# The low half of the shared expert's inner units, made by VectorE in place of GpSimd

## The reference, cut to what matters

```python
# xf: all tokens, layer-normalised; 512 inner values per token
sg = xf @ shared_gate_w.T
su = xf @ shared_up_w.T
shared_out = silu(sg) * su @ shared_down_w.T
# beside it, for each token: 16 scores -> 2 of 4 groups -> 4 experts and their weights
topk_idx, w, _scores = _route(xf, router_w, correction_bias)
```

## Time and profile before

| what | us |
|---|---|
| median of 3 runs | 3146.3 |
| lowest, highest | 3137.9, 3148.9 |
| the profiled execution | 3140.2 |
| its span | 3138.3 |
| PE busy | 2709.5 (86%) |
| VectorE busy | 2195.0 (70%) |
| ScalarE busy | 1759.7 (56%) |
| GpSimd busy | 1983.6 (63%) |
| L1586 on GpSimd, 64 times | median 1.296 each |
| L1483 on VectorE, 64 times | median 0.686 each |

### The profile page before, as it was taken

One profiled execution on the slowest core, in us unless ns is written; L12 is line 12 of the kernel. 1 busy time (PEld: TensorE's weight loads), 2 busy tenths in 40 slices (PEclk: granted clock), 3 DMA queues, 4 the chain that ended last, 5 costly groups with the idle time before them and its releaser, 6 DMA issues. The chain is left out here.

```text
span 3138.3 us, 61611 instructions
## 1 busy us (share of the span) xinstructions
PE 2709.5 (86%) x20082; PEld 2330.9 (74%) x20085; DVE 2195.0 (70%) x5038; ACT 1759.7 (56%) x4605; POOL 1983.6 (63%) x2046
## 2 busy tenths in 40 slices
PE   6999999999999999999978999899994533178887
PEld 5888888888888888888867888788883521056675
DVE  5767677776777767777747767554454559889997
ACT  5666666666666666666643332233332336089997
POOL 4888888888888888888864555500005600068897
PEclk9999999999999999999998999999996655589999
DMA  8666655666565665656561000111114680001111
GB/s 219 116 109 112 112 112 112 113 112 113 112 114 111 115 114 110 114 111 116 106 135 43 29 25 26 41 54 56 59 54 105 170 150 1 14 22 48 48 35 41
DMA packets 710936, 274.99 MB, mean 88 GB/s; under 512 B 606393, under 2 KB 685857, under 8 KB 710626
## 3 DMA queue, kind: packets, MB, share of 16 engines
q1 hardware_dynamic: 704194, 253.19, 40.2%
q0 software_dynamic: 6432, 17.86, 1.7%
HBM read 104.32 MB, written 32.39 MB: 44 GB/s over the span
## 5 line engine op out<-in xcount | busy, mean ns | idle before, releaser
L844 POOL COPY attention_probT<-attention_planesT 128x1024 uint16<-128x1024 uint16 x512 | 677.3, 1368 | 172.9 <-PE attention_turns L422 101.5
L529 ACT ACTIVATE attention_prob<-attention_turns,attention_neg_max 128x256 f32<-128x256 f32 x1024 | 468.6, 483 | 224.6 <-DVE attention_neg_max L682 215.2
L835 POOL COPY attention_planes<-attention_prob 128x1024 uint16<-128x1024 uint16 x512 | 527.5, 1060 | 20.1 <-ACT attention_prob L529 20.1
L682 DVE TENSOR_REDUCE attention_neg_max<-attention_turns 128x2 f32<-128x512 f32 x512 | 317.8, 682 | 176.8 <-PE attention_turns L407 176.3
L383 PE MATMUL attention_turns<-kv_hi,wkv 128*128 128x512 f32 x1024 | 374.2, 406 | 0.0
L351 PE MATMUL attention_turns<-wkv,kv_hi 128*128 128x512 f32 x1024 | 315.5, 389 | 1.9 <-ACT attention_prob L529 1.9
L1804 POOL DMA_INDIRECT far_routed_rows<-rows_out,back_places x64 | 67.3, 1052 | 369.9 <-POOLq L1615 352.7
L422 PE MATMUL attention_turns<-attention_probT,attention_v 128*64 128x128 f32 x4096 | 253.4, 277 | 1.8 <-issue 1.8
L518 ACT COPY attention_v<-attention_turns 128x512 f32<-128x512 f32 x256 | 150.4, 590 | 183.1 <-PE attention_turns L351 182.9
L698 DVE TENSOR_TENSOR attention_turns<-attention_turns,attention_attT_lo 128x512 f32<-128x512 f32 x128 | 139.8, 1092 | 148.1 <-DMA attention_attT_lo<-inverse_rows 146.0
L422 PEld LDWEIGHTS attention_turns<-attention_probT,attention_v 128*64 128x64 f32 x4096 | 222.6, 137 | 19.2 <-issue 2.7
(11 more groups left out here) (361 smaller groups left out, 8075.1 us busy)
## 6 DMA issues: line engine op xcount, KB each, us to landing
attention_attT_lo<-inverse_rows SPq DMA_DIRECT2D x256, 128.0 KB, 3.0
experts_rows<-rows_in SPq DMA_DIRECT2D x69, 132.0 KB, 2.1
rows_out<-experts_down_raw SPq DMA_DIRECT2D x69, 128.0 KB
attention_ctx<-in_ctx SPq DMA_DIRECT2D x32, 256.0 KB, 3.3
attention_planesT<-attention_planes SPq DMA_TRANSPOSE x512, 3.2
far_ctxT<-in_ctxT SPq DMA_DIRECT2D x32, 256.0 KB
weights_ctx<-in_ctx SPq DMA_DIRECT2D x16, 512.0 KB, 3.8
out<-conv_x_out SPq DMA_DIRECT2D x15, 512.0 KB, 2.8
```

What stands on the lines that cost most here:

```text
L529: made = act.activation(prob[n % 2][:, h, :], bank_of("s", 2 * n + e)[:, m * 256:(m + 1) * 256], ACT.Exp, bias=neg_max[:, n % 2, 2 * e + m ...
L682: made = dve.tensor_reduce(neg_max[:, n % 2, 2 * e:2 * e + 2], bank_of("s", 2 * n + e)[:, :].rearrange("p (h c) -> p h c", h=2), AX.X, ALU ...
L835: pool.tensor_copy(planes[n % 2][:, g, :, :], words.rearrange("p (c b) -> p b c", b=2)).then_inc(planes_made, 1)
L844: pool.tensor_copy(words.rearrange("p (c b) -> p b c", b=2), planesT[:, g, :, :]).then_inc(joined, 1)
```

## The change

`low_hidden` moves from GpSimd's program to VectorE's, with the same operation, operands and semaphores. On VectorE it stands behind the weighing of its unit and waits for the high half of the same unit. `measure` moves up, ahead of it.

```diff
+            def low_hidden(n):
+                dve.wait_ge(hid_high, n + 1)
+                tt(hid_lo[n % 3][:, :], weighed[n % 2][:, :], hid_hi[n % 3][:, :].bitcast(F32), ALU.subtract
+                   ).then_inc(hid_split, 1)
...
                 if not n:
                     for m in range(S_DOWN):
                         low_weight(m)
+                if due("measure", n):
+                    measure(due("measure", n))
+                if n < N:
+                    low_hidden(n)
                 if due("picks", n) is not None:
                     route_picks(due("picks", n))
...
                 if due("norm", n):
                     norm(due("norm", n))
-                if due("measure", n):
-                    measure(due("measure", n))
...
-            def low_hidden(n):
-                pool.wait_ge(hid_high, n + 1)
-                pool.tensor_tensor(hid_lo[n % 3][:, :], weighed[n % 2][:, :], hid_hi[n % 3][:, :].bitcast(F32),
-                                   ALU.subtract).then_inc(hid_split, 1)
-
...
             for n in range(N):
-                low_hidden(n)
                 if due("turn1", n):
                     low_x(due("turn1", n))
```

## The result

| | before | after |
|---|---|---|
| median | 3145.4 us (5 runs) | 3161.5 us (5 runs) |
| lowest, highest | 3137.9, 3148.9 | 3160.6, 3167.7 |
| ratio of the times | | 1.0061 [1.0043, 1.0079] |
| profiled execution, its span | 3140.2, 3138.3 | 3166.3, 3164.4 |
| VectorE busy, GpSimd busy | 2195.0, 1983.6 | 2209.0, 1907.7 |

Slower by 0.6%, as forecast (3163.7 us, +0.55%). The ratio is that of the mean times; the two medians lie 16.1 us, 0.51%, apart. The two profiled executions differ by more, 26.1 us, so I cut them where the loop begins and ends: its **start** runs from PE's first gate product to the third rank products (1723.43 us after the change), then come **13 periods** up to the last rank products (2031.10), and the **end**, from there to PE's first product over routed rows (L1183).

What follows compares the result with a forecast made beforehand. Bound: a closed loop of PE's 9.23 and VectorE's 12.53 us per group. Terms 12.2 + 1.2 - 3.8 + 7.8 = +17.4 us on 3146.3 gave 3163.7 us, slower by 0.55%; range 3148 to 3175.

Steps and rivals of the forecast that it cites:

- steady part: Third weighing to rank products, 13 stretches: 2.78 added less 1.84 removed, +0.94 us each, +12.2 us; bounds +10 to +21.
- start: Start of the loop: added low halves delay a down product (+0.6) and the third rank products about as much, +1.2 us.
- end: End of the loop: pad DMAs no longer queue behind GpSimd's low halves and start earlier, -3.8 us; bounds -3 and -7.
- clock: PE's granted clock falls after longer rank waits: 9 of 13 in place of 4, 1.56 us each, +7.8 us.
- The closed loop: A group's period is PE's 9.23 plus VectorE's 12.53 us; anything added between third weighing and picks lengthens every group.
- +1.39 for each low half: On VectorE, what follows the third and fourth weighings comes 1.39 us later, 0.78 of it waiting; +2.78 us a group.
- The stall's -1.84: GpSimd's subtraction queued behind the last scatter DMA holds VectorE's L1388; moving it takes off 1.84 us a group.
- The port: Rival: VectorE's L1448 loses the shared port to GpSimd's low half of x, +7.8 us, 3171.5 us; chance 0.08.
- The idle time: Rival: VectorE's 88 idle us absorb the 39 us of moved work, only the end counts, 3142.5 us; chance 0.09.
- The faster outcome: Rival: a low half adds under 0.92 us, so third weighing to rank products shortens, -18.1 us, 3128.2 us; chance 0.05.

Runs made afterwards that it cites:

- e9_before: The kernel before the change, unchanged, profiled a second time: 3147.4 us, loop 371.69 us.
- e10_after: The changed kernel, unchanged, profiled and compared a second time: 3167.6 us against 3143.5, ratio 1.0073 to the kernel before.
- e1_late: Changed kernel with every low half still on VectorE but last among its unit's steps: 3121.6 us against 3146.9 for the kernel before, ratio 0.9915.
- e6_wait: Kernel before with only each group's third-unit low half on VectorE, directly behind its weighing: 3133.1 us against 3147.2, ratio 0.9961.
- e2_busy: Changed kernel plus 20 matmuls with unread results on PE ahead of each wait for the rank products: 3154.0 us, ratio 1.0017 to the kernel before.
- e4_third: Kernel before with only each group's third-unit low half on VectorE, last in its unit: 3122.2 us, ratio 0.9922.
- e3_copy: Changed kernel plus one unused subtraction on GpSimd behind the scatter of 14 groups: 3202.7 us, ratio 1.0180 to the kernel before.
- e8_busy3: Changed kernel plus 20 unread PE matmuls ahead of rank-product waits, only from the fourth rank products on: 3152.1 us, ratio 1.0014 to the kernel before.
- e5_end: Kernel before with only the last group's four low halves on VectorE, directly behind their weighings: one run, 3142.0 us against 3147.2.

## Why the prediction was right, and where its sizes were off

| term | predicted | measured | measured again (e9_before, e10_after) |
|---|---|---|---|
| steady part, 13 stretches | +12.2 | 168.99 - 158.83 = +10.2 | 168.89 - 158.60 = +10.3 |
| start | +1.2 | 0.0 | +1.0 |
| end | -3.8 | -3.6 | -3.4 |
| clock, 13 stretches from rank products to weighing | +7.8 | 138.68 - 125.98 = +12.7 | 137.14 - 124.44 = +12.7 |
| sum | +17.4 | +19.3 | +20.6 |

The sum came closer than its terms: the steady part was 2 us too high, the clock 5 too low, and that they offset is luck.

- **The closed loop** held. e1_late and e6_wait shortened the stretch and nothing else of weight, and the time followed; e2_busy filled PE's idle time and left the stretch, and only the clock's part came back.
- **+1.39 for each low half** was exact, to 0.01 us, with 0.78 of it waiting; the difference between e6_wait and e4_third, 0.77 us a group, is that wait by itself.
- **The stall's -1.84** was the right mechanism (e3_copy, and L1388 at 175 ns). The mean stretch grew by 0.78 us, not 0.94, just under the lower bound of 0.8. Normalising and the two operations behind it also change: L1388 starts 2.71 us behind the weighing in groups like that of the earlier trace rows and 3.08 in the earlier trace rows, and now 2.71 or 2.83 with the low half's 1.39 taken off, some 0.1 us less in the mean, which I hadn't priced. The last stretch, which has no normalising, grew by 0.64 only.
- **The start** came out at 0.0 in one pair of profiles and +1.0 in the other. The second of its two halves is there: from the down product of the earlier trace rows to the third rank products it is 13.5 us in both profiles after (1709.97 to 1723.43, 1709.71 to 1723.20) and 12.9 in both before, +0.6 as foreseen. The part ahead of that product differs by -0.6 in one pair and +0.5 in the other, though PE waits longer in front of it (5.67 us in both against 4.73 and 4.77). Two pairs can't say whether the first half of the term exists.
- **The clock** is the step that was mis-sized: "at four in six, 9 of 13 would fall". I applied the rate of waits of 1.9 us to waits of 2.5. In the steady part 12 of 12 fell after the change and 11 of 12 in e10_after, against four and three before, so the falls rose by 8, not 5. The range of the term, to +14, held it. The price of a fall, 1.56 us, was right.
- **The rivals.** The port: GpSimd's low half of x begins 2.86 us after the rank products (1820.33), and VectorE's L1448 at 2.15 (1843.44 after 1841.29), in 0.17 us. VectorE was not held there, by the 0.7 us of margin foreseen. The price of that rival was wrong besides: its 2.00 us hold the second unit's 0.61, and the idle time is lessened by the same 0.61 again. Counted once, 4.40 us of delay meet 4.40 of idle time, and the lost port alone would have cost next to nothing. The idle time didn't take the work. The faster outcome needed a low half under 0.92 us; it is 1.39 in the place that the change gave it and 0.61 in that of e1_late, which came out at 3121.6 us where that rival had put 3128.2.

What stays open: what decides, among waits of equal length, which the clock follows; why e8_busy3 repeated only 2 us lower than e2_busy; and where e3_copy's last 6 us lie.

## What to carry to other kernels

An elementwise step moved to a faster engine pays or costs by where it stands in that engine's order: 0.69 us of work behind its producer's hand-over cost 1.39 us in a stretch on which PE waited, and 0.61 or nothing a few instructions later. Find the stretch of the receiving engine without idle time first, and put the new work behind what others wait for. Where one engine's queued work stalls another, move that one piece: one low half in four gave some nine tenths of the best gain seen (ratios 0.9922 and 0.9905). A wait of PE in a full stream of matmuls costs more than its length, 2.5 us of it another 1.56.

## What the runs showed of the hardware

- **A subtraction of GpSimd holds VectorE from before its recorded start.** In the kernel before, the held L1388 starts 0.36 us into the scatter DMA ahead of it and ends 0.04 us after the subtraction. In e3_copy the four normalisings end at 1845.73, 0.81 us after the subtraction's end (1844.92); 1.38 - 0.81 = 0.57 us of their work lay before it, so by this estimate VectorE stood from about 1843.1, 0.5 us ahead of the subtraction's recorded start. Whether the subtraction works before that start, no row shows. An engine's stall can therefore be 1.8 us for a neighbour's 1.3.
- **It holds an instruction with a single tensor input too**: L1370 in e3_copy, and in e9_before L1401, a comparison of a 128x16 tile with a constant, ordinarily 0.17 us:

```profile
1736.65 1.95 DVE L1401 TENSOR_SCALAR experts_group_mask<-experts_group_mask 128x16 f32<-128x16 f32 x1
```

```profile
1736.29 0.96 POOL L1593 DMA_INDIRECT rows_in<-experts_rows,experts_places  x1 [0.30 <-issue]
1737.27 1.28 POOL L1586 TENSOR_TENSOR experts_hidden_lo<-experts_weighed,experts_hidden_hi 128x512 fp32r<-128x512 f32 x1
```

  The Trainium skill (SBUF — State Buffer, section "SBUF: two separate sides") names two SBUF inputs, or the 2-port performance mode, as what makes VectorE contend; whether L1370 and L1401 ran in that mode no row here shows.

- **The clock of PE by the wait ahead of it**, counted from the fourth rank products on in before, after and their repetitions, e5_end, e6_wait and e3_copy: after waits up to 1.68 us, none of 31 was followed by the lower level; after 1.70 the one; after 1.88 to 1.96, 11 of 16; after 2.46 to 2.60, 23 of 24; after 4.10 to 4.16, all 12, with stretches of up to 12.0 us in place of 10.8.
